# Second cross attention: another order of ScalarE's copies and exponentials, VectorE's addition and GpSimd's root

## The reference

```python
def _L1_xattn_ref(q, k, v, mask, w_q, w_k, w_v, w_o):
    def proj(x, w):
        return (x @ w.T).reshape(B, -1, H, D_K).transpose(0, 2, 1, 3)
    query = proj(q, w_q)
    key_ = proj(k, w_k)
    value = proj(v, w_v)
    scores = jnp.einsum('bhqd,bhkd->bhqk', query, key_) / jnp.sqrt(jnp.asarray(D_K, dtype=query.dtype))
    scores = jnp.where(mask == 0, jnp.asarray(NEG, dtype=scores.dtype), scores)
    attn = jax.nn.softmax(scores, axis=-1)
    out = jnp.einsum('bhqk,bhkd->bhqd', attn, value)
    out = out.transpose(0, 2, 1, 3).reshape(B, -1, H * D_K)
    return out @ w_o.T
...
x = x + _L0_ffn_ref(_layernorm(x, axis=-1), L0_ffn_wg, L0_ffn_w1, L0_ffn_w3, L0_ffn_w2)
x = x + _L1_xattn_ref(_layernorm(x, axis=-1), ctx_1024, ctx_1024, mask_1x1xSxS2_ik0, L1_xattn_w_q, L1_xattn_w_k, L1_xattn_w_v, L1_xattn_w_o)
x = x + _L1_ffn_ref(_layernorm(x, axis=-1), ...)
```

## Time and profile before

| what | value |
|---|---|
| median of 3 runs | 1606.81 us (1605.17 to 1607.92) |
| the profiled execution | 1606.48 us |
| its span in the trace | 1604.3 us |
| TensorE busy, share of the span | 91% |
| VectorE busy | 76% |
| ScalarE busy | 70% |
| GpSimd busy | 57% |

### The profile page before, as it was taken

The page is one execution under the profiler, slowest core; times in us unless marked ns, Lnnn a source line. Parts: engine busy times, 40 slices in busy tenths (PEclk is TensorE's granted clock), DMA queues, the critical chain, the costliest instruction groups (busy, mean ns, idle before and its releaser), DMA issues.

```text
span 1604.3 us, 38573 instructions
## 1 busy us (share of the span) xinstructions
PE 1465.3 (91%) x12380; PEld 1212.1 (76%) x12443; DVE 1226.6 (76%) x3032; ACT 1121.2 (70%) x2666; POOL 910.4 (57%) x789
## 2 busy tenths in 40 slices
PE   4899999999888998999996999999898899999988
PEld 3677777777767876777775888888776788888766
DVE  6888888888856557888886788888566778787765
ACT  4888888877754556888784787878633787878732
POOL 4667778777842104555424777777402777777500
PEclk8999999999999997999997999999999999999999
DMA  9800000000012322100000000000000000000000
GB/s 381 330 1 8 11 10 10 10 11 18 11 50 80 85 72 67 35 19 18 17 11 9 14 14 16 14 16 14 10 10 5 7 14 16 13 16 14 10 25 33
DMA packets 75553, 61.29 MB, mean 38 GB/s; under 512 B 40256, under 2 KB 61120, under 8 KB 74688
## 3 DMA queue, kind: packets, MB, share of 16 engines
q1 hardware_dynamic: 71360, 51.69, 10.0%
q0 software_dynamic: 4096, 8.40, 1.8%
HBM read 21.30 MB, written 30.41 MB: 32 GB/s over the span
## 4 chain that ended last, share of the span: by engine, by line
PE 50%; DVE 32%; ACT 8%; issue 6%; POOL 3%; DMA 1%; DVEq 1%; SPq 0%; POOLq 0%; ACTq 0%
PE slot L1642 6%; PE slot L459 5%; PE slot L461 4%; PE slot L460 4%; PE slot L1625 4%; PE slot L1586 4%; PE slot L1660 3%; PE slot L1595 3%; ACT a_p L741 3%; DVE a_sum L859 3%; PE slot L1895 2%; POOL a_rq L1104 2%; DVE c_nm L1427 2%; DVE a_ssq L969 2%; PE slot L1636 2%
## 5 line engine op out<-in xcount | busy, mean ns | idle before, releaser
L1043 POOL TENSOR_TENSOR rs<-mv,nhalf 128x1 f32 (+1 forms) x160 | 98.9, 618 | 232.3 <-DVE mv L1038 165.0
L1811 POOL TENSOR_TENSOR d_A<-d_A,d_B 128x1024 f32<-128x1024 f32 x64 | 150.7, 2355 | 132.2 <-DVE d_B L1749 132.2
L1815 POOL TENSOR_TENSOR d_r<-d_vv,nhalf 128x16 f32<-128x16 f32 x64 | 186.4, 2913 | 46.9 <-DVE d_vv L1771 46.4
L741 ACT ACTIVATE d_p<-slot,d_nm,d_r 128x128 f32<-128x128 f32 x512 | 185.6, 468 | 27.1 <-DVE d_nm L1762 27.1
L741 ACT ACTIVATE a_p<-slot,a_nm,a_rq 128x77 f32<-128x77 f32 x512 | 163.7, 432 | 55.2 <-DVE a_nm L766 55.2
L741 ACT ACTIVATE c_p<-slot,c_nm 128x77 f32<-128x77 f32 x512 | 117.4, 361 | 8.9 <-DVE c_nm L1427 8.8
L1642 PE MATMUL slot<-d_v,d_pT 128*128 128x65 f32 x1024 | 121.8, 272 | 1.7 <-ACT d_pT L1679 1.7
L1642 PEld LDWEIGHTS slot<-d_v,d_pT 128*128 128x128 f32 x1024 | 119.4, 192 | 2.4 <-ACT d_pT L1679 2.1
L748 POOL TENSOR_TENSOR a_p<-a_p,a_rc 128x616 f32<-128x616 f32 x64 | 80.1, 1251 | 70.1 <-DVE a_rc L861 69.6
L1730 DVE TENSOR_TENSOR d_A<-slot,T 128x1024 f32<-128x1024 f32 x64 | 78.3, 1224 | 44.6 <-PE slot L1586 44.6
L1758 DVE TENSOR_REDUCE slot<-slot 128x8 f32<-128x1024 f32 x64 | 78.9, 1233 | 27.8 <-PE slot L1625 25.2
(11 more groups left out here) (288 smaller groups left out, 4531.8 us busy)
## 6 DMA issues: line engine op xcount, KB each, us to landing
routed<-zero SPq DMA_DIRECT2D x2, 9216.0 KB, 49.3
b_x<-routed SPq DMA_DIRECT2D x80, 64.0 KB, 1.8
answers<-b_y SPq DMA_DIRECT2D x40, 128.0 KB, 1.9
X<-in_x SPq DMA_DIRECT2D x2, 1024.0 KB, 7.4
d_zx<-Z SPq DMA_DIRECT2D x64, 32.0 KB
H<-Z SPq DMA_DIRECT2D x64, 32.0 KB
out<-f_o SPq DMA_DIRECT2D x8, 256.0 KB, 2.0
d_zx<-Z SPq DMA_DIRECT2D x64, 31.8 KB
```

The costliest lines, as they stand in the source:

```text
L741: i = e.activation(t["p"][:, h, :], R[slot][:, k // nbank, nk * (k % nbank):nk * (k % nbank) + nk], ACT.Exp, bias=t["nm"][:, h:h + 1], sca ...
L1043: return e.tensor_tensor(rs[:, bass.ds(b, 1)], mv[:, bass.ds(b, 1), 1:2].rearrange("p a b -> p (a b)"), nhalf[:, 0:1], ALU.pow)
L1811: e.tensor_tensor(t["A"][:, p, :], t["A"][:, p, :], t["B"][:, p, :], ALU.add).then_inc(S("d_key"), 1)
L1815: e.tensor_tensor(t["r"][:, it.m(2, 4), :], t["vv"][:, p, :], nhalf[:, 0:16], ALU.pow).then_inc(S("d_key"), 1)
```

## The change

ScalarE's step before: copy of the first half, copy of the second half, exponentials of the first half, projections' copies, exponentials of the second half. Now: copy of the first half, exponentials of the first half, copy of the second half, projections' copies, exponentials of the second half. One small exponential (`warm`) is added in step 3, with which the load of ScalarE's table stands before the projections' copies of step 3 and no longer before the exponentials of step 4.

VectorE's step began with the normalization of b-2 and both `largest`, and ended with addition and statistics of b-6. Now it begins with the first `largest`; then come addition and statistics, of b-7 (one step later), the second `largest` and the normalization. GpSimd's root takes b-7 in place of b-6.

```diff
@@ c_scalar
-                b = it.b(5)
-                if b is not None:
-                    for half in range(2):
-                        e.wait_ge(S(("ac_PTa", "ac_PTb")[half]), count(b, base=NB))
+                if it.static and it.i == 3:
+                    e.activation(warm[:], eps[:, 0, :], ACT.Exp)
+                b4, b5 = it.b(4), it.b(5)
+                for half in range(2):
+                    if b5 is not None:
+                        e.wait_ge(S(("ac_PTa", "ac_PTb")[half]), count(b5, base=NB))
                         e.activation(t["pT"][0:SK, 8 * half:8 * half + 8, :].rearrange("p (a c) t -> p a (c t)", a=2),
                                      R[1][0:SK, :, :], ACT.Copy).then_inc(S(("ac_pTa", "ac_pTb")[half]), 1)
-                b = it.b(4)
-                if b is not None:
-                    p = {"p": t["p"][:, it.m(4, 2), :, :], "nm": t["nm"]}
-                    e.wait_ge(S("ac_mxa"), count(b, base=NB))
-                    exponentials(e, p, 2, 0, 4, SK, S("ac_expa"))
+                    if half == 0 and b4 is not None:
+                        p = {"p": t["p"][:, it.m(4, 2), :, :], "nm": t["nm"]}
+                        e.wait_ge(S("ac_mxa"), count(b4, base=NB))
+                        exponentials(e, p, 2, 0, 4, SK, S("ac_expa"))
@@ c_vector
             def body(it):
+                b = it.b(4)
+                if b is not None:
+                    largest(b, 0, 2)
+                b = it.b(7)
+                if b is not None:
+                    e.wait_ge(S("ac_wo"), count(b, base=NB))
+                    e.tensor_tensor(rows(X, b), rows(X, b), R[0][:, 1:2, 256:384], ALU.add).then_inc(S("ac_add"), 1)
...
+                    stats_tail(e, b, S("ac_bn"), S("ac_ag"), S("ac_ve"), base=NB)
+                b = it.b(4)
+                if b is not None:
+                    largest(b, 1, 3)
                 b = it.b(2)
                 if b is not None:
                     e.wait_ge(S("c_rs"), count(b))
                     layernorm(e, X, t["xn"], b, it.m(2, 2)).then_inc(S("ac_xn"), 1)
-                b = it.b(4)
-                if b is not None:
-                    largest(b, 0, 2)
-                    largest(b, 1, 3)
...
-                if b4 is not None:
-                    e.tensor_tensor(rows(X, b4), rows(X, b4), R[0][:, 1:2, 256:384], ALU.add).then_inc(S("ac_add"), 1)
...
@@ c_pool
-                b = it.b(6)
+                b = it.b(7)
                 if b is not None:
                     e.wait_ge(S("ac_ve"), count(b, base=NB))
                     root(e, b).then_inc(S("ac_rs"), 1)
```

More of the change, by code:

```diff
@@ L1430, in body @@
             def body(it):
+                b = it.b(4)
[5 more added lines that the diff above has]
+                    e.tensor_tensor(rows(X, b), rows(X, b), R[0][:, 1:2, 256:384], ALU.add).then_inc(S("ac_add"), 1)
+                    e.wait_ge(S("ac_add"), count(b, base=NB))
+                    apart(e)
+                    e.bn_stats(st[:, 0, :], rows(X, b)).then_inc(S("ac_bn"), 1)
+                    stats_tail(e, b, S("ac_bn"), S("ac_ag"), S("ac_ve"), base=NB)
+                b = it.b(4)
+                if b is not None:
+                    largest(b, 1, 3)
                 b = it.b(2)
```

## The result

The changed kernel takes 1636.22 us (median of 6 runs, 1629.74 to 1640.09), the kernel before 1604.38 us on the same chips (6 runs, 1601.08 to 1607.92). The ratio is 1.0193, with a 95% interval of 1.0173 to 1.0213: some 31 us. The forecast was 1625.3, in a range of 1613 to 1633. The sign and the loop were right, the size was not; the measured time lies above the range.

A forecast was written before the change was run, and what follows sets the result against it. It took VectorE and TensorE both near 7.1 us, the longest loop through the engines deciding. Loop and split pieces +19.4, seam -1.2, step 4 +0.3 make +18.5 on 1606.5: 1625.0, as median 1625.3, range 1613 to 1633.

The forecast's parts named there:

- The sign and the loop: Whole kernel slower, chance 0.91, because the late second copy closes a loop through TensorE, VectorE and ScalarE of 7.90 us.
- What bounds the kernel before: In the layer's 7.12 us step, VectorE and TensorE are both near 7.1 us; the longest loop through the engines matters.
- The chain of the second copy: ScalarE's second copy starts 1.17 us later; 0.39 is slack, 0.78 lies on the loop: 7.90 us a step.
- VectorE's walk: VectorE's reordered step: second reduction waits about 0.35 us, reciprocal waits for output weights, 0.34 us slack before the first reduction.
- The split pieces: Weight pieces on VectorE before the first reduction, less 0.34 slack: large 1.42, small 0.53, two of each 3.9 us.
- The clock: Rival, much slower: TensorE's clock falls, +4.2 us a step; in a third of the steps +42, 1667; chance 0.05.
- The seam: Between steps 36 and 37, batch 30's addition and statistics move behind the low part TensorE waits for: -1.2 us.
- The first steps: In step 4 normalization moves behind two reductions that wait for TensorE, delaying mixing and key blocks: +0.3 us.
- the table load: ScalarE's earlier table load is worth 0, since ScalarE idles 3.01 us after it before step 4's exponentials; bounds 0 to -0.3.
- faster: Rival: VectorE sets the pace, the filled ScalarE idle time is gain, step about 7.0, total 1602; chance 0.06.
- the half case: Rival: TensorE's 3.32 us stretch shrinks or the reduction is handed on sooner, halving the 0.78: +7, 1613; chance 0.09.
- VectorE as the bound of the regular step: Rival: reordered VectorE instructions wait 0.35 us more for each other, up to +0.3 a step, 1634; chance 0.05.

The follow-up runs named there:

- E7: Kernel before with three more identity transposes on TensorE in every step, ahead of the wait for the second copy: 1610.36 us, ratio 1.0028.
- E1: Changed kernel with ScalarE's order of the kernel before and no early exponential, so only VectorE's and GpSimd's new order: 1603.34 us, ratio 0.9994.
- E3: Changed kernel with 4 of the first half's 8 exponentials ahead of the second copy, the rest behind it: 1604.92 us, ratio 1.0004 against before.
- E4: Changed kernel with 6 of the first half's 8 exponentials ahead of the second copy, the rest behind it: 1619.16 us, ratio 1.007 against before.
- E6: Changed kernel with six identity transposes on TensorE in each step ahead of the wait for the second copy: 1624.58 us, ratio 1.0118 against before.
- E8: E1 with identity transposes where TensorE waits at the layer's start and end (steps 3, 4 and 36): 1602.3 us, ratio 0.9978 against before.
- E9: Kernel before with only E8's identity transposes at the layer's start and end: 1600.91 us, ratio 0.9967 against before.
- E10: The kernel of E8 again with more rounds, on the same chip as E9: 1598.38 us, ratio 0.9951 against before.
- E2: Changed kernel with VectorE's and GpSimd's order of the kernel before, so only ScalarE's new order and early table load: 1687.15 us, single execution.

## Why the prediction was right in its loop and wrong in its size

- *What bounds the kernel before*: right, VectorE and TensorE both lie near 7.1. E7 shows that TensorE's loop sets the step, and E1 that VectorE's order doesn't matter.
- *The chain of the second copy, 7.90 a step, 0.39 us of slack*: right, 7.93 measured, and E3 and E4 fall on the line. It is 0.9 us of the missing 14.6.
- *VectorE's walk*: right. It waits 0.28 us before the first reduction (0.34) and 0.18 before the reciprocal (0.12).
- *The split pieces, 1.42 and 0.53 each*: right. In step 12 the reduction starts at 683.59, where 681.28 + 0.91 = 682.19 would be its time: 1.40. In step 16 the second copy comes 4.70 us after the first in place of 3.40: 1.30. The small ones give 8.34 - 7.93 = 0.41 and 0.42. Together 3.5 for 3.9.
- *The clock*: this is the step that failed. The forecast had it at nothing in its sum. It took the new idle time as an average, 15% of a step, and gave the falling clock a chance of 0.05, as a rival that strikes a third of the steps or none. Its own terms, the wait of 0.78 and the late reduction of 1.42 behind a large piece, add up to a wait of 2.2 us in one step (2.13 measured in step 12), and it never put them together. The new order takes away the cover of 0.39 us, so a delay of VectorE now goes 1 for 1 into one wait of TensorE. In step 6 that is 0.8 us, from two products of the rotary tables that stand ahead of the first reduction in steps 5 and 6, and from a reciprocal that starts late; the forecast had no term for it. In steps 12 and 16 it is the 1.40 and 1.30. The waits grew to 1.56, 2.13 and 2.05 us there, and to 1.54 in step 35, and behind each of them the clock fell. Over 7.93, the pieces and the 0.8, step 6 has 2.3 us, step 7 4.55, step 12 12.18 - 7.93 - 1.40 = 2.85, step 16 1.6 and step 35 1.56: **12.8 us** at the lower clock. The account from step 6 to step 36: 30 x 7.93 = 237.9, pieces 3.5, the late reduction of step 6 0.8, the clock 12.8, together 255.0 of the 255.52 measured; before it was 221.46. E6 shows the clock's share in the other direction, with some 10 us gained by keeping TensorE busy. Both profiles of the changed kernel are from the slow end of its executions, so in the median, which lies 10.9 us over the forecast, the clock's share is likely smaller; how much smaller wasn't measured.
- *What stays open about the clock*: why it falls at one wait and not at another. The rows of before couldn't have said it: its own waits of 1.31 and 1.45 us left the clock at 1.00, and E8 and E9 lost it behind waits of 1.33 to 1.47. What the runs show is that both profiles of the changed kernel lost it in the same five steps, and those of the kernel before, E1, E7 and E10 in none of steps 6 to 35.
- *The seam, -1.2*: the low part starts 1.20 us after the reciprocal, before it was 2.37. Timeline after, then before:

```profile
889.38 0.96 DVE L1491 RECIPROCAL c_rcT<-slot 128x128 f32<-128x128 f32 x1 [6.97 <-PE slot L1383]
...
890.58 0.28 DVE L1739 TENSOR_TENSOR d_hTl<-slot,d_hTh 128x128 fp32r<-128x128 f32 x1
...
890.91 0.80 PE L459 MATMUL slot<-wqkv0h,d_hTl 128*128 128x512 f32 x1 [1.36 <-DVE d_hTl L1739]
```

```profile
855.12 0.96 DVE L1480 RECIPROCAL c_rcT<-slot 128x128 f32<-128x128 f32 x1 [6.19 <-PE slot L1383]
```

  The mechanism was right, but from that reciprocal to the end of the span it is 1638.3 - 889.38 = 748.9, before 1604.3 - 855.12 = 749.2: 0.3 us are left of the 1.2. A part of the loss can be followed, and it is the clock again. In the next layer's second step, the transposes of `d_A` start 26.36 us after the reciprocal (915.74), before 27.18 (882.30): 0.8 us of the lead are left. Then the granted clock is 0.50 in 916 to 918 us, where it was 1.00, and the product of `hTh` (L461) starts 30.27 us after the reciprocal (919.65), before 29.56 (884.68): the lead has become a lag of 0.7. Where the 1.0 us up to the end came back wasn't followed.
- *The first steps, +0.3, and the table load, 0*: step 5 takes 9.32 in place of 9.21, and its first copy starts 0.08 us later (616.76 for 616.68). Right, in so far as nothing is gained.
- *The rivals*: faster didn't come, since the copy started at 3.43 and not by 2.63; the half case didn't either. VectorE as the bound of the regular step didn't come, since it waits 0.28 us; behind the pieces and in step 6 it is the late one, as the forecast had it for the pieces. The clock came, but mixed with the forecast case: a sixth of the steps, not a third or none. It belonged into the sum as a term, with bounds.

The rule of the Trainium skill that the prediction weighed, on a clock that swings when TensorE idles a little between groups ("TensorE: Matmul & The Clock Gate", "A second HAM failure mode: psum-queue depth-cycling"), stood closer to the result than the row it was held against. What the traces show is between the two: the regular 0.23 and 0.76 us in each step left the granted clock at 1.00 over 18 steps in a row (17 to 34), and it fell behind some of the longer waits, of 1.54 to 2.13 us in this kernel, but not behind all such waits (1.81 us in E2's step 14).

## What to carry to other kernels

Before moving an instruction behind another one in an in-order queue, measure its slack: when its reader comes to it, less when it is ready. Up to the slack the move was free here (0.39 us), beyond it it cost 1 for 1, whatever idle time it filled on its own engine. A probe with a part of the work ahead (4, 6, 8 exponentials) shows both sides. A loop through several engines that has used its slack up passes each later delay on as a wait of TensorE. So add the delays that can meet in one step, and give the clock behind the longest waits a term with bounds: none of it, or the 1.6 to 6.8 us that one fall cost here. Take several profiles of each kernel before laying a fall of the clock to a change.

## What the runs showed of the hardware

- TensorE's clock fell after a stretch with 0.51 us of work in 2 us, and was back at 1.00 from 650 us on, though TensorE was busy from 632 us; beside the late copy this cost two steps together 6.8 us. In E2 a stretch with 0.22 us of work in 2 us, around a wait of 1.81 us, left the clock at 1.00, and in E9 it fell behind a wait of 1.33 us. The five slow steps came at the same places in both profiles of the changed kernel. Its times lie between 1629.74 and 1640.09 us, with mean granted clocks from 0.979 to 0.971 (both profiles have 0.971), so an execution can have fewer of them.
- Transposes of the identity, with nobody reading them, made the kernel faster, by 14 us in the changed kernel and by 3 to 7 in the others (E8 and E10 against E1, E9 against before, by their ratios). At 1.2 GHz six of them took 1.48 us, at 2.4 GHz 0.82.
- With TensorE working up to the wait, the weighted values followed the start of the copy sooner (1.10 us for 1.19), and a step was 0.10 us shorter (7.83 for 7.93).
